# Edges in 50 buckets of 250 destinations instead of 30 of 417, in a graph layer with attention and experts

## What is computed

```python
xn = layernorm(x)
x = x + gnn(xn, edges) + linear_attention(xn)      # gnn: two attention convolutions, 4 and 2 heads
x = x + experts(layernorm(x))                       # 8 experts, 2 for each node, and a shared one
```

```python
e = leaky_relu(s_src[src] + s_dst[dst], 0.2)
ee = exp(e - segment_max(e, dst)[dst])
out = segment_sum(ee / segment_sum(ee, dst)[dst] * h[src], dst)
```

## Time and profile before

| | us |
|---|---|
| median of 3 runs | 1655.09 (1655.03 to 1657.01) |
| profiled execution | 1648.37, its span 1646.6 |
| PE busy in the span | 1540.9 (94%) |
| DVE busy | 818.1 (50%) |
| ACT busy, POOL busy | 322.0 (20%), 252.6 (15%) |

### The profile page before, as it was taken

The page is one execution under the profiler, slowest core; times in us unless marked ns, Lnnn a source line. Parts: engine busy times, 40 slices in busy tenths (PEclk is TensorE's granted clock), DMA queues, the critical chain, the costliest instruction groups (busy, mean ns, idle before and its releaser), DMA issues.

```text
span 1646.6 us, 21916 instructions
## 1 busy us (share of the span) xinstructions
PE 1540.9 (94%) x8496; PEld 1024.6 (62%) x8497; DVE 818.1 (50%) x1541; ACT 322.0 (20%) x481; POOL 252.6 (15%) x236
## 2 busy tenths in 40 slices
PE   3999999999898999999989999999999999999994
PEld 3566666557777899999877555444444444444441
DVE  7765347998875799994897433111111111111111
ACT  2111112001223145570273210100000100000000
POOL 1087820000000000000000027111111111111111
PEclk9999999999999999999999999999999999999997
DMA  8900020000003533323111317925628211614315
GB/s 224 380 2 2 2 61 1 1 1 2 1 1 102 148 101 132 88 55 69 46 46 58 144 36 172 336 69 188 221 62 306 95 49 48 215 42 160 98 30 187
DMA packets 84441, 163.79 MB, mean 99 GB/s; under 512 B 18746, under 2 KB 47152, under 8 KB 84105
## 3 DMA queue, kind: packets, MB, share of 16 engines
q1 hardware_dynamic: 65975, 119.07, 22.2%
q0 software_dynamic: 12128, 23.27, 6.1%
q10 hardware_dynamic: 6258, 20.40, 4.4%
HBM read 127.75 MB, written 37.56 MB: 100 GB/s over the span
## 4 chain that ended last, share of the span: by engine, by line
PE 70%; DVE 11%; DMA 8%; issue 4%; SPq 3%; POOL 1%; DVEq 1%; ACT 1%; ACTq 0%; POOLq 0%
PE bank L787 28%; PE bank L1589 5%; PE bank L1550 5%; PE bank L1365 5%; PE bank L1375 5%; PE bank L1457 5%; PE bank L1512 3%; PE bank L697 2%; SPq L368 2%; DVE arena L2249 2%; PE bank L1393 2%; DVE arena L2218 2%; DMA arena<-out_dram,arena 2%; PE bank L1637 1%; DMA arena<-in_x_dram 1%
## 5 line engine op out<-in xcount | busy, mean ns | idle before, releaser
L787 PE MATMUL bank<-arena 128*64 128x384 f32 x3312 | 539.4, 487 | 0.6 <-ACT arena L855 0.6
L787 PEld LDWEIGHTS bank<-arena 128*64 128x64 f32 x3312 | 237.1, 137 | 291.0 <-issue 290.1
L1130 DVE SCALAR_TENSOR_TENSOR arena<-bank,arena 64x384 f32<-64x384 f32 x92 | 52.6, 611 | 379.8 <-DMA arena<-out_dram,arena 232.9
L1589 PE MATMUL bank<-arena 125*125 125x198 f32 (+1 forms) x1200 | 188.8, 316 | 11.5 <-DVE arena L2218 11.4
L1589 PEld LDWEIGHTS bank<-arena 125*125 125x125 f32 x1200 | 181.8, 191 | 16.4 <-DVE arena L2218 16.2
L1550 PE MATMUL bank<-arena 128*125 128x192 f32 x960 | 163.0, 327 | 10.4 <-DVE arena L2171 8.7
L1550 PEld LDWEIGHTS bank<-arena 128*125 128x125 f32 x960 | 155.9, 188 | 12.4 <-DVE arena L2171 10.2
L1260 POOL DMA_INDIRECT slot_table<-arena x80 | 110.4, 1380 | 105.1 <-DMA expert_in<-arena 75.7
L2055 DVE TENSOR_TENSOR arena<-arena,bank 125x417 f32 x186 | 109.4, 588 | 27.5 <-PE bank L1393 19.0
L2249 DVE SCALAR_TENSOR_TENSOR arena<-arena 125x1250 f32<-125x1250 f32 x60 | 90.9, 1516 | 11.6 <-ACT arena L1797 11.6
L654 POOL MEMSET arena<- 1x2500 f32 x1 | 2.2, 2179 | 603.4 <-DVE arena L2201 603.4
(11 more groups left out here) (296 smaller groups left out, 1511.2 us busy)
## 6 DMA issues: line engine op xcount, KB each, us to landing
arena<-in_L_ffn_w_gate_dram SPq DMA_DIRECT2D x9, 2304.0 KB, 9.1
arena<-in_L_ffn_w_up_dram SPq DMA_DIRECT2D x9, 2304.0 KB, 10.5
arena<-in_L_ffn_w_down_dram SPq DMA_DIRECT2D x9, 2304.0 KB, 8.9
arena<-score_rows ACTq DMA_DIRECT2D x18, 585.9 KB
expert_in<-arena SPq DMA_DIRECT2D x23, 384.0 KB, 12.5
arena<-expert_in ACTq DMA_DIRECT2D x23, 384.0 KB, 3.3
arena<-in_L_mix_w_qkv_dram SPq DMA_DIRECT2D x3, 2304.0 KB, 24.1
xn_columns<-arena SPq DMA_DIRECT2D x1, 3750.0 KB, 14.1
```

What stands on the lines that cost most here:

```text
L787: ins = tp.matmul(ps[bank][HP * h:HP * h + HP, 0:384], frm[:, b, k, HP * h:HP * h + HP], ew[h][i][:, k, n * 384:(n + 1) * 384], start=(k = ...
L1589: ins = tp.matmul(ps[bank][0:T, c * width:(c + 1) * width], ptile[0:T, j % NPT, dt * T:(dt + 1) * T], values(n - first, st), start=(st == ...
```

## The change

The destinations are cut into DG = 5 parts of G = 250 instead of 3 of 417: 50 buckets, at most 206 chunks. The rank rounds take RC = 8 edge columns (20 rounds of 400 columns) and go two at a time to ten places, the middle and the end of halves 2 to 6 of the keys and values. The bucket of an edge is found by a multiplication and a shift. 36 instead of 24 chunks ride in the W1 times W2 stage; the other stages keep their number for each product, so the queries carry 90 instead of 82. `counts` is cleared by one ScalarE instruction in front of its fourth key tile, no longer by VectorE. `w2_columns` moves from g = 5, 6 to g = 30, 31. `base0` shares its place with the buffers of the table, since the larger arrays don't fit side by side. The sum of the one-hots starts when four of the five are there. In the diff below the constants come first, then TensorE's program, ScalarE's and VectorE's.

```diff
-    DG = 3
+    DG = 5
-        rank_tmp = take(960).rearrange("p (i c b) -> p i c b", i=2, c=16)
-        RC = 16
+        RC = 8
+        rank_tmp = take(2 * RC * NBK).rearrange("p (i c b) -> p i c b", i=2, c=RC)
+        base0 = words(SMALL + ZB + tab_at, EC * NBK // 2, BF16).rearrange("p (c b) -> p c b", c=EC)
...
-            pe.wait_ge(s_oh, 5)
+            pe.wait_ge(s_oh, 4)
             for b in range(NBK):
                 tp.matmul(ps[4][:, b:b + 1], onehot[0:T, 0:P, b], ones_b[0:T, 0:1], start=True, stop=True)
+            pe.wait_ge(s_oh, 5)
...
+            def edge_ranks(i):
+                if 4 <= i < 4 + RJ // 2:
+                    edge_rank(2 * (i - 4))
+                    edge_rank(2 * (i - 4) + 1)
             def edge_work(g):
                 if g == 0:
                     edge_starts()
-                if 1 <= g < 5:
-                    for j in range(3 * (g - 1), min(3 * g, RJ)):
-                        edge_rank(j)
-                if g == 4:
+                edge_ranks(2 * g + 1)
+                if g == 6:
                     chunk_buckets()
...
                                         wkv[:, 0, k, hf * 384:(hf + 1) * 384], start=(k == 0), stop=(k == KD - 1))
+                        if k == KD // 2 - 1:
+                            edge_ranks(2 * (4 * t + hf))
...
                     w12_product(h, kp)
-                    count_edges(1)
+                    count_edges(2)
                     if h + 1 < H1:
...
             for t in range(NT):
+                if t == 3:
+                    act.wait_ge(s_rankfree, RJ)
+                    act.wait_ge(s_starts, 2)
+                    sc.activation(words(SMALL + COUNTS, CW16)[0:T], zeros[0:T, 0:1].to_broadcast([T, CW16]), ACT.Copy).then_inc(s_cz, 1)
...
-            step(dv.tensor_scalar(dgf[0:T], nd[0:T], float(G), None, ALU.is_ge))
-            step.wait()
-            step(stt(out=dgf[0:T], in0=nd[0:T], scalar=float(2 * G), in1=dgf[0:T], op0=ALU.is_ge, op1=ALU.add))
+            step(dv.tensor_scalar(pi[0:T, 0:EC], nd[0:T], 262.2, None, ALU.mult))
+            step.wait()
+            step(dv.tensor_scalar(ei[0:T, 0:EC], pi[0:T, 0:EC], 16, None, ALU.arith_shift_right))
+            step.wait()
+            step(dv.tensor_copy(dgf[0:T], ei[0:T, 0:EC]))
...
-                if g == 4:
+                edge_ranks(2 * g + 1)
+                if g == 6:
                     edge_slots()
-                    dv.memset(words(SMALL + COUNTS, CW16, I32)[0:T], 0).then_inc(s_cz, 1)
-                if g in (5, 6):
-                    w2_columns(g - 5)
+                if g in (30, 31):
+                    w2_columns(g - 30)
...
                     if h + 1 < H1 and kp == 2:
                         take_w1t(h + 1, 3)
-                    count_edges(2)
+                    count_edges(3)
```

More of the change, by code:

```diff
@@ L80, in gps_layer @@
     assert T * NT == N and T * EC == E and T <= P and G <= 512 and NTM % 2 == 1
-    assert C1 == 2 * C2 and H1 * C1 == D and NCH == 186
+    assert C1 == 2 * C2 and H1 * C1 == D and NCH == 206
     with ExitStack() as ctx:
@@ L108, in gps_layer @@
         zeros = small(D)
-        iota_i = small(G, I32)
+        RW = 417
+        iota_i = small(RW, I32)
         ones_b = small(P, BF16)
@@ L175, in gps_layer @@
         onehot = take(EC * NBK, BF16).rearrange("p (c b) -> p c b", c=EC)
-        base0 = take(EC * NBK, BF16).rearrange("p (c b) -> p c b", c=EC)
         EC1 = EC - P
@@ L216, in gps_layer @@
         NSC = EC - NTB * TC
-        tab_at = 3040
+        tab_at = 2880
+        base0 = words(SMALL + ZB + tab_at, EC * NBK // 2, BF16).rearrange("p (c b) -> p c b", c=EC)
         take = region(ZB + tab_at, 7600 - tab_at)
@@ L239, in gps_layer @@
         ohs = take(2 * OB * T, BF16).rearrange("p (b c n) -> p b c n", b=2, c=OB)
-        ohd = take(4 * 418, BF16).rearrange("p (b n) -> p b n", b=4)
+        ohd = take(4 * G, BF16).rearrange("p (b n) -> p b n", b=4)
         a2bc = take(4 * C2)
@@ L312, in gps_layer @@
         accb = words(SMALL + V12 + NT * D + KD * N + KD * HG, 2 * D).rearrange("p (b n) -> p b n", b=2)
-        route = region(P - SMALL, D + G)
+        route = region(P - SMALL, D + RW)
         lg = route(NT * 9).rearrange("p (t e) -> p t e", t=NT)
@@ L1232, in _ @@
             pl.memset(epst, EPS).then_inc(s_const, 1)
-            step(pl.iota(iota_i, pattern=[[1, G]], base=0, channel_multiplier=0))
+            step(pl.iota(iota_i[:, 0:G], pattern=[[1, G]], base=0, channel_multiplier=0))
             step(pl.memset(tri, 1.0))
@@ L1239, in _ @@
                              pattern=[[-1, P]], channel_multiplier=1).then_inc(s_const, 1)
-            pl.tensor_copy(iota, iota_i).then_inc(s_const, 1)
-            pl.tensor_copy(iota_h[:, 0:G], iota_i).then_inc(s_const, 1)
+            pl.tensor_copy(iota, iota_i[:, 0:G]).then_inc(s_const, 1)
+            pl.tensor_copy(iota_h[:, 0:G], iota_i[:, 0:G]).then_inc(s_const, 1)
             pl.affine_select(out=tri, in_=tri, compare_op=ALU.is_ge, fill=0.0, base=-1,
@@ L1376, in _ @@
                                         wkv[:, 1, k, hf * 384:(hf + 1) * 384], start=(k == 0), stop=(k == KD - 1))
+                        if k == KD // 2 - 1:
+                            edge_ranks(2 * (4 * t + 2 + hf))
                     ins.then_inc(s_vps, 1)
@@ L2019, in _ @@
                     edge_work(4 * t + hf)
-                edge_work(4 * t + 2)
-                edge_work(4 * t + 3)
+                for g in (4 * t + 2, 4 * t + 3):
+                    edge_ranks(2 * g)
+                    edge_work(g)
             dve.wait_ge(s_tbu, NTB)
@@ L2042, in chunk_onehots @@
                 if j % OB == 0:
-                    step(dv.tensor_tensor(ohs[:, (j // OB) % 2], iota_h[:, 0:T].unsqueeze(1).to_broadcast([P, OB, T]),
-                                          srow[:, j:j + OB].unsqueeze(2).to_broadcast([P, OB, T]), ALU.is_equal))
+                    nb = min(OB, NCH - j)
+                    step(dv.tensor_tensor(ohs[:, (j // OB) % 2, 0:nb], iota_h[:, 0:T].unsqueeze(1).to_broadcast([P, nb, T]),
+                                          srow[:, j:j + nb].unsqueeze(2).to_broadcast([P, nb, T]), ALU.is_equal))
                 dv.tensor_scalar(ohd[:, j % 4, 0:G], iota_h[:, 0:G], dcol[:, j:j + 1], None, ALU.is_equal)\
```

7 lines of the change are left out of this document (2 added, 5 removed).

## The result

The changed kernel takes 1672.06 us (median of 4 runs, 1668.65 to 1674.87), the kernel before beside it 1656.05 (4 runs, 1655.03 to 1657.68). The ratio is 1.0097, 95% interval 1.0080 to 1.0114: slower by 1%, 8.6 us above the 1663.5 forecast and 1.1 above the top of its range (1651 to 1671). The profiled execution took 1669.5 us with a span of 1667.8 (before 1648.4 and 1646.6).

The account below looks back on a forecast made before the run. TensorE was taken to bound most stages before 492 us, VectorE the two where TensorE idles. Terms 0.4 + 8.0 + 1.3 + 11.9 - 5.6 - 7.6 = +8.4 on the 1655.1 median gave 1663.5 us, range 1651 to 1671.

Parts of the forecast that it names:

- Opening: Before TensorE's transposes: larger one-hots and one more bucket instruction make the last statistics 0.4 us late; bounds 0 and 0.9.
- Ranks and tables: Keys and values stage: longer bases and twenty rank rounds +8.0 us (bounds +7.0 to +9.5), wider table products +1.3.
- Hidden parts: Scatters, ScalarE's clearing of the counts and the moved W2 columns: all covered by other work, 0 us.
- W1 times W2: Stage with 36 chunks: adds stay 0.87 us apart, held by offset loads, and borders lengthen; +11.9 us, bounds +6 to +13.
- First-layer product: Its stage: 80 chunk products at 250 columns take 0.107 us instead of 0.177, saving 5.6 us, or 5.3.
- Queries: Query stage: shorter adds and one-hots cut periods to 11.56 us; -7.6 us, bounds -4 to -15.4.
- Behind: After 492 us: nothing changes, since the mask and both attention layers read the same counts.
- the adds follow the engine: Rival, chance 0.17: adds 0.63 us apart instead of 0.87 in the W1 and query stages; +1.6, 1656.7 us, no change.
- the forecast's 0.33 + 0.22: A chunk's add and one-hot on VectorE in us by the skill's cycle table, below the queue's 0.87.
- The slower rival: Ranks at 0.85 us a round (+12 with tables), W1 stage +13, queries only -5: +15, 1670 us; chance 0.11.

Follow-up runs that it names:

- a3_fixed: The changed kernel with each add's offset fixed in the program text, without load or register steps, so counts land wrongly: 1648.71 us, ratio 0.9979.
- c_after_noassert: The changed kernel with the offset load kept but its two bounding register instructions left out: 1659.2 us, ratio 1.0018.
- c_after_multi2: The changed kernel without the bounding register instructions and with one load bringing the offsets of two chunks: 1660.21 us, ratio 1.0034.

## Why the prediction was right in sign and low in size

- **Opening, +0.4:** the first transpose starts at 29.46 instead of 29.01. Right.
- **Ranks and tables, +9.3:** the stage grew by 9.8. The bases took 8.47 and 1.80 us, the first wait was to be 1.9 and was 1.6 (line below), rounds were 0.79 apart, the table group 1.43 us where the earlier trace rows has 1.29. Right.

```profile
51.19 0.38 PE L1310 MATMUL bank<-arena 125*125 125x400 bf16 x1 [1.59 <-DVE arena L1951]
```

- **Hidden parts, 0:** nothing of them is late. ScalarE's clearing took 5.40 us where the forecast had 6.1 (in proportion to the earlier trace rows it would be 6.7). The first scatter started at 89.37, when the slots were ready, and not at 82.24; the last one ended at 228.8 (before 222.1), ahead of TensorE's 242.5.

```profile
89.37 1.26 POOL L1261 DMA_INDIRECT slot_table<-arena  x1 [83.28 <-issue]
...
109.48 5.40 ACT L1696 ACTIVATE arena<-arena 125x6251 f32<-125x6251 f32 x1
```

- **W1 times W2, +11.9:** it was +20.2. This term fell, in its size. Its mechanism, the pace of 0.87 from add to add, is in the rows, and so are the longer borders. What was wrong is a silent assumption: every TensorE duration in the walk came from rows at a clock of 1.00. At that clock the walk holds to 2 or 3 us: the kernels with spare products show 47.5 and 48.5, +13.7 and +14.7, with their own spare work in it. So even at the full clock the stage may have lain a little over the term's upper bound of +13. The remaining 6.5 or more came from the 1.2 GHz level, at which a product of eight passes takes 2.85 instead of 1.58 and stands on the path between two VectorE copies.
- **First-layer product, -5.6:** -5.5, periods of 2.21. Right.
- **Queries, -7.6:** -6.6. Periods were 11.8 in the mean (11.4 to 12.2) where 11.56 was walked. TensorE still waited for one-hots, 6.3 us where the earlier trace rows has 8.7:

```profile
PE bank L1403 <- DVE arena L2066: 6.3, 9, 1.3
```

- **Behind:** +2.9 in the profiled pair, within the scatter of that stretch; the bias between the stages -0.1.

Sum: 0.5 + 9.8 + 20.2 - 0.1 - 5.5 - 6.6 + 2.9 = 21.2, the difference of the spans; 16.0 by the medians, because the profiled execution of the kernel before was 7.7 under its median and the changed kernel's 2.6. By the spans the sum was forecast at 8.4 and is 21.2, so 12.8 were missing: 8.3 in W1 times W2, 2.9 in the scatter behind, 1.0 in the queries, the rest in small parts. By the medians 7.6 of the 8.6 us are the sum's, and 1.0 is the base, since the median before is 1656.05 now and was 1655.1. The bounds of the terms reached +17, so 1672; the range stopped one short of that. A top of 1672 would have been right in number only, as no bound had the clock in it.

Of the rivals, "the adds follow the engine" was wrong for this kernel: they do so in a3_fixed, where the engine's own pace is 0.52 and not the 0.63 that the forecast gave it. By the Trainium skill (VectorE: DVE Perf Modes, The DRAIN you can't avoid) the next instruction is paced by the one before it; a3_fixed agrees, with its 0.33 behind an add and 0.19 behind a one-hot. The changed kernel at 0.87 doesn't, because there the queue is the slower one, and c_after_noassert with 0.62 lies between. Of the forecast's 0.33 + 0.22 only the 0.22 of the one-hot comes from the page's cycles; the 0.33 is that of the rows. The slower rival, 1670, came nearest in number, for a reason that it didn't name: it put ranks and queries worse than they were.

I had named what it costs TensorE to wait, but not what waiting does to the speed of its next product. The view that would have warned was the busy share of TensorE by stretch: 29.5 of 35.0 before, and by my own walk the same work plus twelve short products in 47 us. With that share the clock could be doubted, and a rival of +7 us belonged beside the sum. This case's trace has 0.50 granted between 266 and 282 us, in a stage in which TensorE's gaps before its products are 1.7 us at most. The busy share alone would have been a doubt and no proof, since c_after_multi2 held its clock at 28.9 of 42.8. The Trainium skill (TensorE: Matmul & The Clock Gate, A second HAM failure mode: psum-queue depth-cycling) tells of a kernel whose TensorE idles briefly but often between groups and whose gate swings between its two levels; this stage agrees.

## What to carry over

Before small work is moved into a stage with idle TensorE, ask what the idle time will be afterwards: work that waits on another engine lengthens the stage without filling it, and TensorE may then run its own work there at half speed. Price each chunk at the slower of the engine's time and the time of its queue (load of an offset, register steps, address), since making tiles smaller shortens only the first; cut the queue's part before cutting the tile. And when a small change of order gives back much, look at the clock on both sides before you credit the order: one count moved behind the turns gave back 8.0 us of the stage, but 1.8, with cheap loads, where the clock was 1.00 on both sides.

## What the runs showed of the hardware

- TensorE's granted clock fell to its 1.2 GHz level in the middle of a stage in which it had worked 3.1 of 4 us and then 2.2 of 4 us; it came back to 0.96 and 1.00 behind two pieces with 3.24 of 4 us, while TensorE was no busier (3.05 and 2.37 of 4 us). The same instructions took it 38.6 us there and 28.8 in a3_fixed. The mean busy share of the stage doesn't tell which it will be: a3_fixed had 28.8 of 40.8 at 1.00, c_after_multi2 28.9 of 42.8 at 1.00, and c_after_noassert had 0.80 with the same products.
- Three spare products for a unit were enough to hold the clock, and made the stage shorter by 6.5 us although TensorE's busy time at the full clock is 8.2 us higher with them (37.1 against the 28.9 of c_after_multi2).
- An add whose offset stands in the program starts 0.19 us behind the one-hot in front of it, one whose offset comes from a register 0.29 at the least (a3_fixed, c_after_noassert), with no idle time shown.
- A load of two offsets into registers takes 0.52 us, of one 0.30. The two bounding register instructions (0.19 and 0.02) cost 0.25 us of each add with 250 columns and, with loads in pairs, 0.08 with 417.
- The same 1142 us of later work took up to 10.8 us more in other executions.
